# A two-layer graph kernel: its block is closed without GpSimd's drain, and small work around the end of the first layer is moved

## The reference, cut to what matters

```python
# layer 0
Q = (V[src] @ Wq + bq);  K = (V[dst] @ Wk + bk);  Vv = (V[dst] @ Wv + bv)      # heads of 16
scores = einsum(Q, K) / sqrt(16) + (E @ Wb + bb)
alpha = softmax of scores within each dst;  Hagg = segment_sum(alpha * Vv, dst)
x1 = layernorm(x + Hagg @ Wo + bo)
# layer 1
h = x1 @ W;  e = leaky_relu((h @ a1)[src] + (h @ a2)[dst], 0.2)
out = layernorm(x1 + segment_sum(softmax(e)[:, None] * h[src], dst))
```

## Time and profile before

| what | value |
|---|---|
| median of 3 runs | 1059.08 us (1057.36 to 1061.64) |
| the profiled execution's own time | 1056.71 us |
| its span, first to last instruction | 1055.0 us |
| mean granted TensorE clock | 0.84 of 2.4 GHz |
| busy share: POOL, DVE, ACT, PE | 72%, 77%, 67%, 63% |
| moved by DMA | 196.90 MB, mean 187 GB/s |

### The profile page before, as it was taken

One profiled execution on the slowest core, in us unless ns is written; L12 is line 12 of the kernel. 1 busy time (PEld: TensorE's weight loads), 2 busy tenths in 40 slices (PEclk: granted clock), 3 DMA queues, 4 the chain that ended last, 5 costly groups with the idle time before them and its releaser, 6 DMA issues.

```text
span 1055.0 us, 14618 instructions
## 1 busy us (share of the span) xinstructions
PE 662.7 (63%) x3270; PEld 448.6 (43%) x3270; DVE 807.1 (77%) x3723; ACT 705.4 (67%) x2036; POOL 761.1 (72%) x801
## 2 busy tenths in 40 slices
PE   0467777777787677787655656656566555556640
PEld 0246555555565555565444545545432111111110
DVE  4789999999988798896876666666548777777760
ACT  3659998999899797997423444534447666666650
POOL 6777777777777777777077777777737777777775
PEclk9979998999889898988868787878858788778775
DMA  7666786787767678657348777887743322332310
GB/s 200 197 190 200 222 278 210 237 264 231 226 220 238 213 222 258 202 194 226 122 140 285 254 255 248 277 271 248 222 132 93 96 85 86 88 94 85 88 43 25
DMA packets 82013, 196.90 MB, mean 187 GB/s; under 512 B 19814, under 2 KB 22005, under 8 KB 81916
## 3 DMA queue, kind: packets, MB, share of 16 engines
q1 hardware_dynamic: 56774, 148.35, 43.3%
q0 software_dynamic: 25152, 47.63, 16.0%
HBM read 122.71 MB, written 77.22 MB: 190 GB/s over the span
## 4 chain that ended last, share of the span: by engine, by line
POOL 42%; issue 19%; DVE 15%; DMA 8%; ACT 8%; PE 7%; DVEq 1%; SPq 0%; POOLq 0%; ACTq 0%
POOL xs L484 24%; POOL h_res L484 16%; ACT xsT L888 5%; DMA xs<-x_all,row_tab 4%; DVE nst L1408 4%; DVE node_out L1390 4%; POOL out_dram L488 2%; DMA h_res<-in_x,dst_tab 2%; DVE match L1041 1%; DVE part L1395 1%; DVE nmv L1416 1%; ACT logs L898 1%; PE psum L674 1%; PE psum L680 1%; PE psum L597 1%
## 5 line engine op out<-in xcount | busy, mean ns | idle before, releaser
L484 POOL DMA_INDIRECT xs<-x_all,row_tab x196 | 187.7, 958 | 86.9 <-issue 83.0
L488 POOL DMA_INDIRECT out_dram<-yb,at_last x196 | 195.1, 995 | 76.1 <-issue 54.2
L484 POOL DMA_INDIRECT xs<-in_x,src_tab x196 | 187.0, 954 | 61.7 <-issue 58.8
L484 POOL DMA_INDIRECT h_res<-in_x,dst_tab x196 | 187.3, 956 | 59.7 <-issue 59.7
L725 ACT ACTIVATE h_res<-node_in,shift,rstd 128x128 f32<-128x128 f32 (+1 forms) x392 | 155.7, 484 | 0.3 <-DVE shift L1168 0.3
L700 PE MATMUL psum<-node_out,ident_inv 128*128 128x512 f32 x98 | 73.1, 836 | 97.5 <-DVE node_out L1390 97.5
L866 ACT ACTIVATE xsT<-psum 128x512 f32<-128x512 f32 x48 | 28.7, 597 | 145.5 <-PE psum L680 145.2
L1390 DVE SCALAR_TENSOR_TENSOR node_out<-node_out,same_prev,xsT 128x128 f32<-128x128 f32 x196 | 68.6, 350 | 48.5 <-ACT xsT L888 36.2
L725 ACT ACTIVATE yb<-psum,shift,rstd 128x128 f32<-128x128 f32 x196 | 73.6, 455 | 29.2 <-DVE shift L1401 26.5
L552 PE MATMUL psum<-h_res 128*128 128x512 f32 x98 | 59.3, 690 | 41.9 <-ACT h_res L732 41.8
L680 PE MATMUL psum<-ident,xs 128*128 128x128 f32 x192 | 39.8, 344 | 72.7 <-DMA xs<-x_all,row_tab 72.6
(11 more groups left out here) (279 smaller groups left out, 1806.9 us busy)
## 6 DMA issues: line engine op xcount, KB each, us to landing
x1d_in<-x_all SPq DMA_DIRECT2D x98, 256.0 KB, 3.9
node_in<-in_x SPq DMA_DIRECT2D x48, 512.0 KB, 4.3
x_all<-h_res SPq DMA_DIRECT2D x48, 512.0 KB
out_dram<-node_out SPq DMA_DIRECT2D x48, 512.0 KB, 3.3
x_all<-yb SPq DMA_DIRECT2D x49, 256.0 KB, 2.6
src_b<-src_t SPq DMA_DIRECT2D x49, 256.0 KB, 7.3
node_in<-x_all SPq DMA_DIRECT2D x24, 512.0 KB, 5.8
h_res<-in_edge_attr SPq DMA_DIRECT2D x7, 784.0 KB
```

The source lines that it names most:

```text
L484: return pool.indirect_dma_start(out=to, out_offset=None, in_=table, in_offset=bass.IndirectOffsetOnAxis(ap=idx, axis=0))
L488: return pool.indirect_dma_start(out=table, out_offset=bass.IndirectOffsetOnAxis(ap=idx, axis=0), in_=rows, in_offset=None, bounds_check=l ...
```

## The change

- The block is opened with no_gpsimd_drain=True: at its end the engines meet by semaphores, and GpSimd executes no drain.
- The seven loads of source numbers go out one for each pass, s = 20 to 26, no longer all in pass 45. reach_of(0) and reach_of(1) move from the code for group 48 to the ends of passes 46 and 47.
- apply_nodes(END) is split: four rows of it at the end of ScalarE's pass 47, four in the code for group 48 behind the copy of xfT. SP stores the chunk in pass 49, behind the edge rows of group 45 and ahead of the three loads of node rows for stage 2 (load_late, L396).
- CAPS 3 and 4 are groups 36 to 41 (run in pass 42) and 42 to 47 (in the code for group 48).
- For groups 46 to 48 the variance comes from four bn_aggr (row_variances) and no longer from five small operations, and the shift from their mean.
- The last group's outputs go to bank 6 (tiles 0 and 1) and bank 5 (tiles 2 and 3). ScalarE scales the first two, ahead of x1f, VectorE the other two; last_applied counts to 2.

```diff
+    SOURCES = 20
-    CAPS = ((0, 12), (12, 24), (24, 36), (36, 44), (44, 48), (48, GROUPS))
+    CAPS = ((0, 12), (12, 24), (24, 36), (36, 42), (42, 48), (48, GROUPS))
-        block = ctx.enter_context(nc.Block())
+        block = ctx.enter_context(nc.Block(no_gpsimd_drain=True))
+        def last_bank(t):
+            return 6 if t < G // 2 else 5
@@ sync
-                        sp.wait_ge(last_applied, 1)
+                        sp.wait_ge(last_applied, 2)
-                k = s + AHEAD - 4
-                if edge(k):
+                k = END if s == END + 1 else s + AHEAD - 4
+                if edge(k) and (k < END or s == END + 1):
                     sp.wait_ge(x1_applied, k + 1)
                     move_nodes(node_chunk(x1_all, k), node_x1[0:parts(k), k % NX, :], k, x1_stored[k % NX])
-                if s == GROUPS - 4:
+                if s == SOURCES:
                     sp.wait_ge(turn_out, 32)
-                    for r in range(SB):
-                        load_sources(sp, r)
+                if SOURCES <= s < SOURCES + SB:
+                    load_sources(sp, s - SOURCES)
@@ tensor
-                if g == END:
-                    mm(bank[6], ident[:, :], xd[:, g % XD, :], start=False, stop=False)
+            def last_outputs():
+                half = G // 2 * D
+                for b, cols in ((bank[6], slice(0, half)), (bank[5], slice(half, GW))):
+                    mm(b[:, cols], ones_bf[:, :], bias_parts[:, 1, :].unsqueeze(1).to_broadcast([96, G // 2, D]),
+                       start=True, stop=False)
+                    mm(b[:, cols], ident[:, :], xd[:, END % XD, cols], start=False, stop=False)
+                pe.wait_ge(hv_turned, GROUPS)
+                for t in range(G):
+                    last = mm(tile(bank[last_bank(t)], t), tile(hT[:, END % 2, :], t), wo[:, :], start=False,
+                              stop=t % (G // 2) == G // 2 - 1)
+                last.then_inc(o_mm, 1)
-            outputs(END)
+            last_outputs()
@@ scalar
-                if s == TAIL:
-                    apply_nodes(END)
+                if s == END - 1:
+                    apply_nodes(END, HALVES[0])
             act.wait_ge(fix_pe, 1)
             fn(xfT[:, :], bank[2][:, 0:P], ACT.Copy).then_inc(fix_act, 1)
+            apply_nodes(END, HALVES[1])
             weights(END)
...
             fn(frs[:, 0:1], flog[:, :], ACT.Exp, scale=-0.5).then_inc(fix_act, 1)
+            act.wait_ge(shift_done, nth(END))
+            act.wait_ge(x1d_stored[END % YB], use(END - YB, YB) * 16)
+            scale_rows(yb[:, END % YB, :], bank[6], P, range(G // 2), rstd[:, nth(END) % 2, :], shift[:, nth(END) % 2, :])\
+                .then_inc(last_applied, 1)
             act.wait_ge(fix_dve, 7)
@@ vector
+            def row_variances(b):
+                dve.wait_ge(y_stats, b + 1)
+                for t in range(G):
+                    last = v.bn_aggr(nmv[:, b % 2, t, :], nst[:, t, :])
+                last.then_inc(var_done, 1)
-                    if s == hi + (hi == CAPS[-2][0]):
+                    if s == hi:
                         cap_block(b)
                 products(s)
+                reach_of(s - TAIL)
             attr_products(END)
             attr_sums(END)
-            reach_of(0)
...
-            variances(END - 2)
+            row_variances(END - 2)
             cap_block(len(CAPS) - 2)
-            reach_of(1)
...
-            variances(END - 1)
+            row_variances(END - 1)
...
-            variances(END)
+            row_variances(END)
...
-            for t in range(G):
+            for t in range(G // 2, G):
                 u = nth(END) % 2
-                last = v.tensor_scalar(tile(yb[:, END % YB, :], t), tile(bank[6], t), ...
+                last = v.tensor_scalar(tile(yb[:, END % YB, :], t), tile(bank[5], t), ...
```

More of the change, by code:

```diff
@@ L745, in deviations @@
                 if not edge(b + AHEAD):
-                    fn(logs[:, 0:G], spread[:, 4, 0:G], ACT.Ln, bias=eps_cols[:, 0:1]).then_inc(log_done, 1)
+                    var = nmv[:, b % 2, :, 1] if b >= TAIL else spread[:, 4, 0:G]
+                    fn(logs[:, 0:G], var, ACT.Ln, bias=eps_cols[:, 0:1]).then_inc(log_done, 1)
                     act.wait_ge(log_done, nth(b))
@@ L780, in copy_weighted, with apply_nodes @@
                 fn(hT[:, g % 2, :], bank[7], ACT.Copy).then_inc(hv_turned, 1)
-            def apply_nodes(k):
+            def apply_nodes(k, rows=range(ROWS)):
                 n, u = parts(k), nth(k - AHEAD) % 2
@@ L786, in apply_nodes @@
                     act.wait_ge(x1_stored[k % NX], landed(k - NX, NX))
-                scale_rows(node_x1[0:n, k % NX, :], node_in[0:n, k % NI, :], n, range(ROWS),
-                           rstd[:, u, G:NR], shift[:, u, G:NR]).then_inc(x1_applied, 1)
+                last = scale_rows(node_x1[0:n, k % NX, :], node_in[0:n, k % NI, :], n, rows,
+                                  rstd[:, u, G:NR], shift[:, u, G:NR])
+                if rows.stop == ROWS:
+                    last.then_inc(x1_applied, 1)
             for s in range(FIRST, TAIL):
@@ L1125, in row_moments @@
                     dve.wait_ge(y_done, g + 1)
-                rows = bank[6] if g == END else yb[:, g % YB, :]
                 for t in range(G):
+                    rows = bank[last_bank(t)] if g == END else yb[:, g % YB, :]
                     last = v.bn_stats(nst[:, t, :], tile(rows, t))
@@ L1165, in shifts @@
                 dve.wait_ge(rstd_done, nth(b))
+                width = NR if edge(k) else G
                 if edge(k):
                     v.tensor_tensor(ratio[:, k, :], rstd[:, u, NR:NR + ROWS], dev[:, u, :], ALU.mult)
-                v.scalar_tensor_tensor(shift[:, u, :], spread[:, 0, :], -0.5, rstd[:, u, 0:NR], ALU.mult, ALU.mult)\
-                    .then_inc(shift_done, 1)
+                if b >= TAIL:
+                    v.scalar_tensor_tensor(shift[:, u, 0:G], nmv[:, b % 2, :, 0], -1.0, rstd[:, u, 0:G], ALU.mult, ALU.mult)\
+                        .then_inc(shift_done, 1)
+                else:
+                    v.scalar_tensor_tensor(shift[:, u, 0:width], spread[:, 0, 0:width], -0.5, rstd[:, u, 0:width],
+                                           ALU.mult, ALU.mult).then_inc(shift_done, 1)
+            def row_variances(b):
[3 more added lines that the diff above has]
+                last.then_inc(var_done, 1)
             def cap_block(b):
@@ L1324, in _ @@
             dve.wait_ge(x1d_stored[END % YB], use(END - YB, YB) * 16)
-            for t in range(G):
+            for t in range(G // 2, G):
                 u = nth(END) % 2
-                last = v.tensor_scalar(tile(yb[:, END % YB, :], t), tile(bank[6], t), rstd[:, u, t:t + 1], shift[:, u, t:t + 1],
+                last = v.tensor_scalar(tile(yb[:, END % YB, :], t), tile(bank[5], t), rstd[:, u, t:t + 1], shift[:, u, t:t + 1],
                                        ALU.mult, ALU.add)
```

## The result

The kernel after takes 1044.49 us (median of six runs, five of them between 1043.72 and 1045.41; the sixth took 1880.03 us and is left out of the ratio), the kernel before 1058.25 in the runs beside it (1056.60 to 1061.64). The ratio is 0.9871, with a 95% interval from 0.9848 to 0.9894: 1.3% less time, clear of the noise, by 11 to 16 us. The profiled executions are 1056.71 us (span 1055.0) before and 1044.38 us (span 1042.6) after, 12.3 us apart.

What follows compares the result with a forecast made beforehand. GpSimd was taken to set the pace of all three stages. Gains of 6.3 us at the block's end and 4.1 at the end of stage 1 made 10.4, so 1059.08 - 10.4 = 1048.7 us, range 1045.5 to 1055.7.

Steps and rivals of the forecast that it cites:

- The end: End of the block: without GpSimd's drain the barrier closes at 1048.7 us, a gain of 6.3 us, perhaps nothing.
- The end of stage 1: Hole after the first gathers: x1f store and GpSimd's next gather come earlier by 3.6 + 0.3 + 0.2 = 4.1 us.
- if the weighted values come 3.3 us earlier (3.2 for the node rows and a little of the landing): Group 47's weighted values, end of stage 1: with them 3.3 us earlier, products(48) start at 505.35, 3.7 us earlier.
- group 45 already waits for its rows: Pass 45: moving cap_block to pass 42 frees it, but group 45 waits for rows anyway; no gain in the sum.
- the last gather's landing as the limit: End of stage 1: last gather lands at 502.0, group 48's turn is 3.06 us earlier, the least gain for products(48).
- The queue to products(48): VectorE from group 47's weighted values to products(48): 5.26 us shrinks to 4.85 through reach_of, variances and a larger cap_block.
- Variances and last rows: Fix-up chain behind products(48): variances(47) give 0.3 us, splitting the last tiles' scaling between ScalarE and VectorE 0.2.
- The covers: Stage 1: moved node rows fit ScalarE's waits of 1.99 and 3.46 us; GpSimd's 17.5 us distance covers the source loads.
- rival E: Stage 1: mid-stage source loads hold up the engines until GpSimd runs out of buffers; slower, 1082 us, chance 0.05.
- rival C: End of stage 1: the last gather lands late, costing 3.4 of the 4.1 us; 1052.1 us, chance 0.12.
- The base: Whole kernel: the 10.4 us sum was subtracted from the median 1059.08, with the profiled execution 2.4 us below it.
- the range's lower end: Whole kernel: 1045.5 us, from the full 6.3, 4.7 of the tail and 2 us of scatter between runs.

## Why the forecast was 4.2 us too high

**The end: right.** 6.3 forecast, 6.23 in the traces, behind the last scatter 7.90 us with the drain and 1.66 to 1.73 without, in every trace but one of the 1290 us. There it is 2.77, and the time outside the span 0.7 where it is 1.7 to 1.8 in all others, so that the two together are the same. The Trainium skill (Runtime: NRT & Kernel Launch, The ~15µs preamble/postamble breakdown) has a barrier of the runtime behind the kernel that waits for all engines. That it would collect the same wait is not borne out: 1.7 us outside the span in the kernel before, 1.7 in the kernel after and 1.8 in the run of the drain alone.

**The end of stage 1: the sum low, and its parts wrong.** The step that failed is "if the weighted values come 3.3 us earlier (3.2 for the node rows and a little of the landing)". They came 4.24 us earlier, and the shares are nearly the other way round: 2.41 up to the turn of group 46 (484.19 for 486.60), 1.39 with the clock behind it, which the prediction didn't have, and 0.4 from the node rows. Of the 2.41, 1.4 are the late landing (the run of the drain alone has this turn at 485.18), and the other 1.0 is pass 45 without segment ends: from products(45) to turn_dst(46) it is 5.91, 5.92 and 5.91 us in the three traces with the segment ends there and no late landing (the drain alone, sources and node rows, source loads alone), and 4.90 in the kernel after (479.29 to 484.19). The prediction gave this nothing ("group 45 already waits for its rows"). The landing was in the chain of the earlier trace rows at 7.75 us and was priced at next to nothing, because I took the last gather's landing as the limit for all that lies behind; this limit exists (501.67 for the 502.0 forecast), but the path behind it is 2.75 us long and not the 4.02 that I let it have, so products(48) could come 4.66 us earlier, not 3.6. Why the node rows' 3.2 us on the chain gave 0.4 is in the chain of the kernel after, between products(46) and products(47):
```profile
487.16 0.76 DVE h_res L1091
487.97 1.06 PE psum L572 x8
489.26 0.89 PE psum L566 x8
490.15 0.44 PE psum L551 x4
490.81 0.89 PE psum L590 x8
491.70 0.88 PE psum L560 x2
492.60 0.46 ACT h_res L784
493.18 0.60 ACT h_res L747
493.83 1.14 PE psum L556 x2
495.07 0.75 DVE h_res L1091
```
TensorE's own queue of scores, values, source turn, outputs and queries, with two copies of ScalarE and the keys, takes this turn 7.91 us, at full clock, without ScalarE's node rows. With them it was 8.34 (the run of the drain alone). The second path lay 0.4 us below the first.

**The queue to products(48): right.** 4.84 us for 4.85. But it hardly decides: the run of sources and node rows, with the old queue of 5.26 us, has products(48) at the limit of the last gather too. The run with the segment ends cut as before, which should have shown this by itself, gave no verdict.

**Variances and last rows: 0.88 for 0.5.** The new variances count twice. The prediction had those of group 47 (0.3, measured 0.40), and not those of group 48, which stand in VectorE's queue between the fix-up and the last rows: 0.44. The split of the last rows gave 0.23 for 0.2, and 0.19 is lost again: from the issue of the x1f store to the first gather it is 3.94 us in the kernel before (523.54 to 527.48) and 4.13 after (517.81 to 521.94), and it is 3.9 in every such trace with the old last rows and 4.1 in every one with the new. Why stays open. These parts are read from the traces; neither ran alone.

**The covers: right.** The source loads of passes 20 to 26 cost GpSimd nothing: no gather of stage 1 but the very first, which waits 2.3 us in both kernels, has an idle time above 0.4 us before it, so rival E is gone. So is rival C: group 48 is turned at 501.67, not beyond 503.

**The base: the largest part.** The prediction summed against the profiled execution, saw that this lay 2.4 us below the median of before, and subtracted its sum from the median, as if the kernel after would have the same distance. It hadn't: its profiled execution (1044.38) is its median. Of the 2.4 us, 0.8 is the median before itself, 1059.08 by three runs and 1058.25 by six. That most of the rest is the late landing, which comes later in some executions than in the profiled one, is argued: the same loads give holes of 24.80 and 28.04 us and a spread of 5.4 us in the kernel after, which without them lies within 1.7 us; but no trace of a longer execution of the kernel before was taken. In numbers: 2.4 from the base, 1.4 from the end of stage 1 (5.54 for 4.1), 0.55 from GpSimd's later phases, less 0.1 for the end (6.23 for 6.3) and 0.1 between the profiled execution after and the median: 4.2 us. The last 0.55 are within what the same program does: the second hole is 14.1 to 15.9 us in these traces.

Three slips of the prediction change nothing in this: the terms named for the range's lower end (6.3, 4.7 and 2 us) add up to 1046.1 and not 1045.5, rival E's sum is 1082.7 and not 1082, and at the end four engines wait for GpSimd, which is the fifth.

What stays open is why the clock falls. On the chips of 1059 us, in the three traces in which group 46 lands late, TensorE's wait of 1.8 to 3.7 us is followed by a granted clock of 0.50, and in the four in which it doesn't, keys(46) take 1.1 us at 1.00. But elsewhere the two don't go together: ahead of turn_dst(44) the run with the source loads alone waits 1.74 us for a DMA and has its keys at full clock behind it, while the kernel before has them at half clock behind 1.58; and keys(45) take 2.05 us in the timed run with the loads late, with no wait for a DMA ahead. That the stop is the cause was argued, not shown.

## What to carry to other kernels

A stretch of work on the chain is worth what separates it from the next path, not its length: 3.2 us of ScalarE gave 0.4, because TensorE's queue was as long but for that. Loads that nobody needs yet are not free where a gather must land: seven of 256 KB cost 3 to 6 us in the hole, and most of the spread between runs came with them. When a change takes away something whose size differs between executions, the gain over the median can be larger than in one trace (here 13.8 against 12.3 us); read the spread of before as a part of the question, and compare phases of the traces, not single times.

## What the runs showed of the hardware

- GpSimd's drain ends some 7.7 us behind its last scatter. Without it the span ends 6.2 us earlier, and these do not reappear outside the span (1.7 to 1.8 us with the drain and without, in every trace but one).
- The landing of the same gather, in the same program, differs between executions by enough to move the end of a stage by 2 us (a hole of 27.49 and of 25.34 us with the same stage 1); with seven 256 KB loads ahead of it it took 7.75 and 7.94 us.
- On four of the seven chips that the experiments came to, every kernel here took 1281 to 1302 us, in the median or in a single run, with waits of ScalarE, VectorE and TensorE that no other engine or DMA of the core is seen to end (125 us ahead of VectorE's scores in the trace with five spare matmuls, none in the kernel before at 1056.71); there GpSimd waits in nearly every turn of stage 1, and a gain of 5 us at its holes wasn't seen.
